# The second bias of the experts, added from a broadcast row by VectorE instead of a product on TensorE

## The chip, the cores and the metric

One core of one Trainium2 chip runs the kernel. The metric is the device time of one execution in microseconds (us), the median of several runs. Five engines work side by side and meet only at semaphores: TensorE (PE), VectorE (DVE), ScalarE (ACT), GpSimd (POOL) and SyncE (SP), which here only issues transfers.

## The reference, cut to what matters

4096 tokens of 256 features pass a graph layer over a 4096 x 4096 adjacency and then a mixture of 16 experts, of which each token uses two:

```python
h = gelu(xf @ W1[e] + b1[e])          # 256 -> 512
o = h @ W2[e] + b2[e]                 # 512 -> 256
y = y + combine[:, e:e + 1] * o       # combine: the token's weight for expert e
```

## The kernel before

**Stages.** A first stage loads and normalises the tokens (to about 54 us of the profile). A second goes through 32 tiles of 128 tokens: adjacency times features on TensorE, the graph layer, the router, and two rows per token (features, token number, weight) written to a list in DRAM that is sorted by expert (to about 380 us). The third stage, which the change is about, takes that list in `BLOCKS` = 79 blocks of 128 rows, each block of one expert, and adds the results to the output in DRAM.

**A step of the third stage.** Every engine runs its own `bstep(q, r)` for block b = 8q + r, in a fixed order, and works on different blocks at once:

- PE: `hidden(b)` (6 products of 512 columns, L530), `tokens_T(b+1)` (4 transposes, L510), `hidden_T(b-1)` (4 transposes, L538), `expert_out(b-2)` (L547 and 12 products of 256 columns, L553).
- DVE: `copy_tokens_T(b+1)` (L1032), `bias1(b)` (L1041), `cut_low(b-1)` (L1047), `weigh(b-2)` (L1055), and in odd steps of the first 32 `cut_low_late` (L1062).
- ACT: `gelu(b)` (L709), `cut_high(b-1)` (L715), and in odd steps of the first 32 `cut_high_late` (L705).
- SP: in odd steps `load_late` (L382, 512 KB of weights), then `load_block(b+4)` (L377, 136 KB of rows).
- POOL: `add_results(b-2)` (L1231, an indirect transfer that adds to the output).

Products are made in fp16 with every factor cut in a high and a low part. The weights of experts 0 to 7 are cut during the second stage; those of experts 8 to 15 are the 16 "late" halves, cut in the odd steps of blocks 1 to 31: ACT writes the high part, then DVE, which waits for it, the low part. SP waits for that low part before it loads the next weights into the same buffer.

**The second bias** is one more product at the head of `expert_out`: its stationary operand is a column of `sel`, broadcast, that picks expert e, and its moving operand is `b2hl`, which holds the high parts of all 16 biases in 16 partitions and the low parts in 16 others. `b2hl` and `sel` are made once in the first stage: a load on SP, a memset and a cut on DVE (L771, L814), a copy on ACT (L669), a memset and two selections on POOL (L1125, L1128), and one more transfer on SP (L352) ahead of its first weight load, which waits for the cut. `weigh` then multiplies by the token's weight while it copies out of PSUM.

Of the kernel before, what the change touches and what calls it, by code (L numbers as in the profile page):

```python
# [37 lines left out]
P = 128  # L38
N = 4096
D = 256  # L40
E = 16
# [40 lines left out]
def build(nc, x, adj, gnn_W, gnn_b, Wr, br, W1, b1, W2, b2, out):  # L82
    ctx = ExitStack()

    def sb(name, shape, dt):
        return ctx.enter_context(nc.sbuf_tensor(name, shape, dt))

    def sem(name):
        return ctx.enter_context(nc.semaphore(name))
# [40 lines left out]
    brb = sb("brb", [P, E], F32)  # L130
    b2s = orows[0:E, 6, :]
    b2l = orows[0:E, 3, :].bitcast(F16)[:, 0:D]
    b2hl = sb("b2hl", [P, D], F16)
    sel = sb("sel", [P, E], F16)
    id32 = sb("id32", [P, P], F32)
# [90 lines left out]
    a_in = [sem(f"a_in{k}") for k in range(AB)]  # L226
    w_in = [sem(f"w_in{k}") for k in range(2)]
    w_late = [sem(f"w_late{k}") for k in range(2)]
    listed = [sem(f"listed{c}") for c in range(2)]
# [22 lines left out]
    def load_x(eng, c, b):  # L252
# [4 lines left out]
              (wr[:, :, :], Wr.rearrange("(c p) n -> p c n", p=P)),  # L257
              (b2s, b2),
              (gb, gnn_b.rearrange("(a d) -> a d", a=1).broadcast_to([P, D])),
# [62 lines left out]
    def _(sp):  # L322
# [20 lines left out]
        def step(i, k):  # L343
            t = tile(i, k)
            if is_(t, lambda t: 3 <= t < T + 3):
                store_base(i, k - 3)
            if isinstance(t, int) and t == T:
                load_b1()
            if isinstance(t, int) and t == 0:
                sp.wait_ge(ev("b2_cut"), 1)  # L350
                after(sp, "b2_zeros", 0)
                sp.dma_start(b2hl[E:2 * E, :], b2l).then_inc(ev("b2_in"), 16)  # L352
            if k % 2 == 0 and is_(t, lambda t: t < T):
                which = k // 2
                if is_(i, lambda i: i >= 1):
                    sp.wait_ge(ev("w_cut"), i * 2 + which - 1)
                sp.dma_start(staged(which, which), w_dram(i, which)).then_inc(w_in[which], 16)
# [26 lines left out]
        AHEAD = 4  # L384

        def bstep(q, r):
            if late(q, r) is not None and late(q, r) + 2 < 2 * (E - EARLY):
                load_late(late(q, r) + 2)
            nxt = shift(q, r, AHEAD)
            if exists(*nxt):  # L390
                load_block(*nxt)
# [13 lines left out]
    def _(pe):  # L405
# [135 lines left out]
        def expert_out(q, r):  # L541
            e = expert[r] if r < U - 2 else expert_of(q, r)
            after(pe, "low_cut", blk(q, r))
            if not isinstance(q, int) or blk(q, r) >= 2:
                after(pe, "weighted", blk(q, r) - 2)
            n = 0
            pe.matmul(q_o[r % 2][:, 0:D], sel[:, bass.ds(e, 1)].broadcast_to([P, P]), b2hl[:, :], start=True, stop=False)  # L547
            for c in range(HC):
                high, low = hh[:, r % 2, c * P:(c + 1) * P], hl[:, r % 2, c * P:(c + 1) * P]
                wh = wall[:, bass.ds(w_at(e, 1, 0) + c * D, D)]  # L550
                wl = wall[:, bass.ds(w_at(e, 1, 1) + c * D, D)]
                for a, w in ((high, wh), (high, wl), (low, wh)):
                    mm = pe.matmul(q_o[r % 2][:, 0:D], a, w, start=False, stop=n == 3 * HC - 1)  # L553
                    n += 1
            mm.then_inc(ev("expert_out"), 1)
# [11 lines left out]
        pe.wait_ge(ev("table_made"), 1)  # L567
        pe.wait_ge(ev("b2_in"), 16)
        pe.wait_ge(ev("sel_made"), 3)
        tokens_T(0, 0)  # L570
# [16 lines left out]
    def _(act):  # L587
# [34 lines left out]
        def scale_base(i, k):  # L622
            r = tile(i, k)
            if is_(r, lambda r: r >= 2):
                act.wait_ge(base_out[k % 2], pair(i, k) * 16)
            if isinstance(r, int) and r < 2:
                act.wait_ge(ev("b2_in"), 16)
            after(act, "base_scale", r)
            after(act, "base_shift", r)
            act.activation(base[k % 2], x1, ACT.Identity, scale=bs[:, 0:1], bias=bs[:, 1:2]).then_inc(ev("base_made"), 1)  # L630
# [36 lines left out]
        act.activation(wg[:, 0, :, :], wg_arrival, ACT.Copy, scale=SW).then_inc(ev("wg_high"), 1)  # L667
        after(act, "b2_zeros", 0)
        act.activation(b2hl[0:E, :], b2s, ACT.Copy, scale=SW).then_inc(ev("b2_high"), 1)  # L669

# [40 lines left out]
        def cut_high(q, r):  # L711
# [3 lines left out]
            act.activation(hh[:, r % 2, :], q_g[r % 2][:, :], ACT.Copy, scale=SH).then_inc(ev("high_cut"), 1)  # L715

        def bstep(q, r):
            prev = shift(q, r, -1)
            if exists(q, r):
                gelu(q, r)  # L720
            if exists(*prev):
                cut_high(*prev)
            if late(q, r) is not None:
                cut_high_late(late(q, r))
# [5 lines left out]
    def _(dve):  # L730
# [39 lines left out]

        V.memset(b2hl[:, :], 0.0).then_inc(ev("b2_zeros"), 1)  # L771
        V.memset(gb_ones[:, :], SX * SW / 2.0 / SG / (P // 2)).then_inc(ev("gb_ones"), 1)
# [25 lines left out]
        for c in range(1, XC):  # L798
# [13 lines left out]
                               op0=ALU.mult, op1=ALU.subtract).then_inc(ev("gb_cut"), 1)  # L812
        after(V, "b2_high", 0)
        V.scalar_tensor_tensor(out=b2l, in0=b2s, scalar=SW, in1=b2hl[0:E, :],  # L814
                               op0=ALU.mult, op1=ALU.subtract).then_inc(ev("b2_cut"), 1)

# [232 lines left out]

        def weigh(q, r):  # L1050

            after(V, "expert_out", blk(q, r))
            if not isinstance(q, int) or q > 0:
                after_added(V, q - 1, r)
            V.tensor_scalar(orow[r], q_o[r % 2][:, 0:D], info[r][:, 1:2].bitcast(F32), None, ALU.mult)\  # L1055
             .then_inc(ev("weighted"), 1)

# [9 lines left out]
        def bstep(q, r):  # L1067
            prev, prev2, nxt = shift(q, r, -1), shift(q, r, -2), shift(q, r, 1)
            if exists(q, r):
                e = expert_of(q, r)  # L1070
            if exists(*nxt):
                copy_tokens_T(*nxt)
            if exists(q, r):
                bias1(q, r, e)
            if exists(*prev):
                cut_low(*prev)
            if exists(*prev2):
                weigh(*prev2)
            if late(q, r) is not None:
                cut_low_late(late(q, r))  # L1080
# [5 lines left out]
    def _(pool):  # L1086
# [37 lines left out]
        L.iota(pad[:, D:D + 1].bitcast(I32), [[0, 1]], base=N, channel_multiplier=1).then_inc(ev("pad_made"), 1)  # L1124
        L.memset(sel[:, :], 0.0).then_inc(ev("sel_made"), 1)  # L1125
        for k in range(2):
            L.wait_ge(ev("sel_made"), 1 + k)
            L.affine_select(out=sel[:, :], in_=sel[:, :], compare_op=ALU.not_equal, fill=SH, base=-E * k,  # L1128
                            pattern=[[-1, E]], channel_multiplier=1).then_inc(ev("sel_made"), 1)

        def rstd0(c):
# [139 lines left out]
```

## Time and profile before

| | |
|---|---|
| median of 3 runs | 705.9 us (705.65 to 708.77) |
| the profiled execution, time | 704.46 us |
| its span (first to last instruction) | 702.5 us |
| granted clock of TensorE, mean over the span | 0.971 |
| PE, DVE, ACT, POOL busy | 83%, 69%, 33%, 51% |

The span is what the trace covers; 1.96 us of the profiled execution lie around it. Busy shares are means over stages with different limits, so they don't say which engine sets a stage's pace.

### The profile page before, as it was taken

The numbers are of one execution on the slowest core, as the hardware profiler recorded it, in microseconds if no ns is written. First come the engines' busy times: TensorE is split into PE (matmuls) and PEld (weight loads), VectorE is DVE, ScalarE is ACT, GpSimd is POOL, SyncE is SP. The second block draws the span as 40 slices with busy tenths as digits, with TensorE's granted clock in tenths as the row PEclk, the third lists the DMA queues.
The fourth block names the chain that finished last, engine by engine and source line by source line (L and its number), as shares of the span: only waits on it lengthen the run. The fifth ranks groups of instructions, "written<-read, shape, count | busy, mean of one in ns | idle before, by whom it ended". The sixth has DMA issues, their size and how long they took to land.

```text
span 702.5 us, 17495 instructions
## 1 busy us (share of the span) xinstructions
PE 585.0 (83%) x4798; PEld 454.3 (65%) x4799; DVE 486.3 (69%) x1430; ACT 229.1 (33%) x440; POOL 361.8 (51%) x392
## 2 busy tenths in 40 slices
PE   0009999999999999999972479999999999999993
PEld 0007888788887788788862156666667677776772
DVE  2794788888888888888875156766665555555552
ACT  2260323333333332333322034443443233232331
POOL 4473367566675666666435734444443444444444
PEclk9999999999999999999995599999999999999997
DMA  9549688899888888899254335676654444444420
GB/s 266 112 73 192 117 162 180 184 178 185 169 181 179 154 170 176 182 183 182 82 170 172 133 105 124 132 152 145 134 107 77 77 76 70 66 73 68 75 41 0
DMA packets 65915, 93.21 MB, mean 133 GB/s; under 512 B 9547, under 2 KB 40559, under 8 KB 65360
## 3 DMA queue, kind: packets, MB, share of 16 engines
q0 software_dynamic: 33696, 51.87, 44.5%
q1 hardware_dynamic: 31024, 38.72, 17.4%
q10 hardware_dynamic: 1152, 2.10, 0.9%
q8 instruction: 21, 0.34, 0.2%
q14 instruction: 22, 0.18, 0.1%
HBM read 103.71 MB, written 25.83 MB: 184 GB/s over the span
## 4 chain that ended last, share of the span: by engine, by line
PE 40%; DVE 29%; issue 18%; POOL 6%; DMA 2%; DVEq 2%; ACT 2%; POOLq 1%; SPq 0%; ACTq 0%
PE bank L530 13%; PE bank L553 13%; DVE at_xg L781 7%; PE bank L538 4%; PE bank L510 2%; DVE wall L839 2%; DVE bst L849 2%; DVE orows L846 2%; POOL rows L1216 2%; PE bank L473 2%; PE bank L421 2%; PE bank L475 2%; DVE xf L865 1%; DVE xseT L832 1%; PE bank L547 1%
## 5 line engine op out<-in xcount | busy, mean ns | idle before, releaser
L473 PE MATMUL bank<-wall,at_xg 128*128 128x257 f16 x1024 | 238.1, 275 | 0.0
L475 PE MATMUL bank<-wall,at_xg 128*128 128x256 f16 x1024 | 237.9, 275 | 0.0
L1231 POOL DMA_INDIRECT out_dram<-orows,at_xg x79 | 125.1, 1584 | 164.5 <-DMA out_dram<-orows,at_xg 113.5
L530 PE MATMUL bank<-wall,feat 128*128 x474 | 117.0, 383 | 10.0 <-issue 8.0
L1047 DVE SCALAR_TENSOR_TENSOR wg<-bank,xseT 128x512 f16<-128x512 f32 x79 | 54.6, 691 | 92.2 <-ACT xseT L715 92.2
L473 PEld LDWEIGHTS bank<-wall,at_xg 128*128 128x128 f16 x1024 | 103.6, 101 | 13.3
L475 PEld LDWEIGHTS bank<-wall,at_xg 128*128 128x128 f16 x1024 | 100.9, 99 | 13.3
L709 ACT ACTIVATE hgs<-hgs 128x512 f32<-128x512 f32 x79 | 49.8, 630 | 181.7 <-DVE hgs L1041 181.7
L553 PE MATMUL bank<-wall,xseT 128*128 x632 | 108.1, 273 | 0.0
L781 DVE STREAM_TRANSPOSE at_xg<-abuf 128x512 int32<-128x512 int32 x128 | 89.4, 699 | 20.3 <-DMA abuf<-in_adj_dram 10.5
L1197 POOL DMA_INDIRECT rows<-feat,posi x64 | 68.2, 1066 | 50.1 <-issue 49.7
L553 PE MATMUL bank<-wall,wg 128*128 x316 | 86.1, 273 | 0.0
L530 PEld LDWEIGHTS bank<-wall,feat 128*128 128x128 f16 x474 | 46.1, 98 | 57.8 <-issue 23.4
L248 POOL DMA_DIRECT2D abuf<-in_adj_dram x128 | 72.7, 584 | 11.2 <-DVE at_xg L781 9.3
L1184 POOL TENSOR_TENSOR feat<-xf,feat 128x512 f16<-128x512 f32 x32 | 37.2, 1161 | 73.0 <-ACT feat L619 73.0
L553 PEld LDWEIGHTS bank<-wall,xseT 128*128 128x128 f16 x632 | 61.7, 98 | 8.5
L1041 DVE SCALAR_TENSOR_TENSOR hgs<-bank,abuf 128x512 f32<-128x512 f32 x79 | 53.7, 680 | 0.0
L1032 DVE COPY feat<-bank 128x512 f16<-128x512 f16 x79 | 33.3, 422 | 25.8 <-PE bank L510 23.9
L619 ACT ACTIVATE feat<-xf 128x512 f16<-128x512 f32 x32 | 20.2, 631 | 94.3 <-DVE xf L865 88.8
L538 PE MATMUL bank<-id,hgs 128*128 128x128 f32 x316 | 48.0, 274 | 0.7 <-ACT hgs L709 0.7
L715 ACT ACTIVATE xseT<-bank 128x512 f16<-128x512 f32 x79 | 45.8, 579 | 0.3 <-PE bank L538 0.3
L502 PE MATMUL bank<-firsts,ones 128*128 128x16 f16 x1 | 0.2, 173 | 54.3 <-DVE gbm L811 54.3
(153 smaller groups left out, 835.9 us busy)
## 6 DMA issues: line engine op xcount, KB each, us to landing
abuf<-in_adj_dram POOLq DMA_DIRECT2D x128, 256.0 KB, 6.0
wst<-in_L_ffn_W_dram SPq DMA_DIRECT2D x32, 512.0 KB, 4.8
at_xg<-rows SPq DMA_DIRECT2D x79, 136.0 KB, 2.4
out_dram<-orows SPq DMA_DIRECT2D x32, 128.0 KB
abuf<-in_L_ffn_b_dram SPq DMA_DIRECT2D x4, 1024.0 KB, 10.5
wall<-in_x_dram ACTq DMA_DIRECT2D x8, 256.0 KB, 8.8
wall<-in_x_dram SPq DMA_DIRECT2D x8, 256.0 KB, 8.0
out_dram<-orows,at_xg POOLq DMA_INDIRECT x79
```

The lines of the kernel that those rows point to most:

```text
L248: eng.dma_start(arrived[b * PQ:(b + 1) * PQ, k % AB, :, :], adj_v[bass.ds(pair(i, k), 1), k % 2, b, :, :, :].rearrange("n i a c -> i (n a) ...
L473: both = [lambda: pe.matmul(ps_acc[odd][:, 0:D + 1], w, xh[:, j, 0:D + 1], start=j == 0, stop=j == T - 1), lambda: pe.matmul(ps_acc[odd][: ...
L475: lambda: pe.matmul(ps_acc[odd][:, 0:D], w, xl[:, j, :], start=False, stop=False)]
L530: mm = pe.matmul(q_h[r % 2][:, :], a, w, start=n == 0, stop=n == 3 * DC - 1)
L538: mm = pe.transpose(q_g[r % 2][:, c * P:(c + 1) * P], hg[r % 2][:, c * P:(c + 1) * P], id32[:, :])
L553: mm = pe.matmul(q_o[r % 2][:, 0:D], a, w, start=False, stop=n == 3 * HC - 1)
L709: act.activation(hg[r % 2], hg[r % 2], ACT.Gelu).then_inc(ev("gelued"), 1)
L781: V.transpose(at[:, c, :].bitcast(I32).rearrange("p (n a i) -> p a n i", a=Q, i=PQ), arrived[:, k % AB, :, c * CW // CH:(c + 1) * CW // CH ...
L1041: V.scalar_tensor_tensor(out=hg[r % 2], in0=q_h[r % 2][:, :], scalar=1.0 / (SX * SW), in1=b1all[:, bass.ds(e * H, H)], op0=ALU.mult, op1=A ...
L1047: V.scalar_tensor_tensor(out=hl[:, r % 2, :], in0=q_g[r % 2][:, :], scalar=SH, in1=hh[:, r % 2, :], op0=ALU.mult, op1=ALU.subtract).then_i ...
L1197: L.indirect_dma_start(rows, at_place, feat[:, odd, k, :], None).then_inc(listed[odd], 16)
L1231: L.indirect_dma_start(out, bass.IndirectOffsetOnAxis(ap=info[r][:, 0:1].bitcast(U32), axis=0), orow[r], None, bounds_check=N - 1, oob_is_ ...
```

## The change

PE's bias product, `sel` and `b2hl` go, with all that made them. SP gets `load_b2(b-1)` at the head of its step b: it reads the block's expert from the table, waits until `summed` of block b-3 is there (the buffer is one of two) and loads that expert's row of `b2` from DRAM into all 128 partitions, 128 KB in SBUF. DVE's `weigh` becomes `add_b2`: it waits for the row and adds it, scaled, to PE's result on its way out of PSUM. The weight is now applied by ACT, in place, in a new `weigh(b-2)` that stands in ACT's step behind `cut_high(b-1)` and ahead of `cut_high_late`. PE waits for `summed` instead of `weighted` before it reuses a bank; POOL still waits for `weighted`.

```diff
-    b2s = orows[0:E, 6, :]
-    b2l = orows[0:E, 3, :].bitcast(F16)[:, 0:D]
-    b2hl = sb("b2hl", [P, D], F16)
-    sel = sb("sel", [P, E], F16)
+    b2row = [feat[:, k, 1, 0:D] for k in range(2)]
...
-              (b2s, b2),
...
-            if isinstance(t, int) and t == 0:
-                sp.wait_ge(ev("b2_cut"), 1)
-                after(sp, "b2_zeros", 0)
-                sp.dma_start(b2hl[E:2 * E, :], b2l).then_inc(ev("b2_in"), 16)
...
+        def load_b2(q, r):
+
+            e = sp.value_load(tab[0:1, bass.ds(blk(q, r) + P, 1)], min_val=0, max_val=E - 1)
+            if not isinstance(q, int) or blk(q, r) >= 2:
+                after(sp, "summed", blk(q, r) - 2)
+                passed(sp)
+            sp.dma_start(b2row[r % 2], b2[bass.ds(e, 1), :].broadcast_to([P, D])).then_inc(b2_in[r % 2], 16)
+
         def bstep(q, r):
+            if exists(*shift(q, r, -1)):
+                load_b2(*shift(q, r, -1))
...
-                after(pe, "weighted", blk(q, r) - 2)
+                after(pe, "summed", blk(q, r) - 2)
             n = 0
-            pe.matmul(q_o[r % 2][:, 0:D], sel[:, bass.ds(e, 1)].broadcast_to([P, P]), b2hl[:, :], start=True, stop=False)
...
-                    mm = pe.matmul(q_o[r % 2][:, 0:D], a, w, start=False, stop=n == 3 * HC - 1)
+                    mm = pe.matmul(q_o[r % 2][:, 0:D], a, w, start=n == 0, stop=n == 3 * HC - 1)
...
-            if isinstance(r, int) and r < 2:
-                act.wait_ge(ev("b2_in"), 16)
...
-        act.activation(b2hl[0:E, :], b2s, ACT.Copy, scale=SW).then_inc(ev("b2_high"), 1)
...
+        def weigh(q, r):
+
+            after(act, "summed", blk(q, r))
+            act.activation(orow[r], orow[r], ACT.Copy, scale=info[r][:, 1:2].bitcast(F32)).then_inc(ev("weighted"), 1)
+
         def bstep(q, r):
-            prev = shift(q, r, -1)
+            prev, prev2 = shift(q, r, -1), shift(q, r, -2)
             if exists(q, r):
                 gelu(q, r)
             if exists(*prev):
                 cut_high(*prev)
+            if exists(*prev2):
+                weigh(*prev2)
             if late(q, r) is not None:
                 cut_high_late(late(q, r))
...
-        V.memset(b2hl[:, :], 0.0).then_inc(ev("b2_zeros"), 1)
...
-        V.scalar_tensor_tensor(out=b2l, in0=b2s, scalar=SW, in1=b2hl[0:E, :],
-                               op0=ALU.mult, op1=ALU.subtract).then_inc(ev("b2_cut"), 1)
...
-        def weigh(q, r):
+        def add_b2(q, r):
 
             after(V, "expert_out", blk(q, r))
+            V.wait_ge(b2_in[r % 2], (q * (U // 2) + r // 2) * 16 + 16)
             if not isinstance(q, int) or q > 0:
                 after_added(V, q - 1, r)
-            V.tensor_scalar(orow[r], q_o[r % 2][:, 0:D], info[r][:, 1:2].bitcast(F32), None, ALU.mult)\
-             .then_inc(ev("weighted"), 1)
+            V.scalar_tensor_tensor(out=orow[r], in0=b2row[r % 2], scalar=SH * SW, in1=q_o[r % 2][:, 0:D],
+                                   op0=ALU.mult, op1=ALU.add).then_inc(ev("summed"), 1)
...
-        L.memset(sel[:, :], 0.0).then_inc(ev("sel_made"), 1)
-        for k in range(2):
-            L.wait_ge(ev("sel_made"), 1 + k)
-            L.affine_select(out=sel[:, :], in_=sel[:, :], compare_op=ALU.not_equal, fill=SH, base=-E * k,
-                            pattern=[[-1, E]], channel_multiplier=1).then_inc(ev("sel_made"), 1)
```

## Rows read from the trace of the kernel before

**Rows 1.** The page's first part: busy time, share of the span, instructions.

```profile
PE 585.0 (83%) x4798; PEld 454.3 (65%) x4799; DVE 486.3 (69%) x1430; ACT 229.1 (33%) x440; POOL 361.8 (51%) x392
```

**Rows 2.** Windows of the third stage: length, busy us (instructions) per engine, clock, DMA share, GB/s.

```profile
404.00:412.00 8.00, 3.72 (x27) 2.49 (x28) 3.78 (x6) 2.63 (x5) 2.36 (x3) 1.00 0.23 55
...
426.00:518.00 92.00, 86.22 (x660) 60.08 (x657) 63.16 (x111) 38.11 (x60) 40.44 (x26) 1.00 0.64 140
518.00:680.00 162.00, 158.69 (x1233) 114.13 (x1231) 97.15 (x185) 52.24 (x93) 71.28 (x46) 1.00 0.42 72
```

**Rows 3.** Timeline of DVE, ACT and SP, two steps: start, duration, instruction, idle before.

```profile
460.33 0.68 DVE L1041 SCALAR_TENSOR_TENSOR hgs<-bank,abuf 128x512 f32<-128x512 f32 x1
...
461.05 0.63 ACT L709 ACTIVATE hgs<-hgs 128x512 f32<-128x512 f32 x1 [2.08 <-DVE hgs L1041]
...
461.58 0.58 ACT L715 ACTIVATE xseT<-bank 128x512 f16<-128x512 f32 x1
...
462.06 1.05 ACT L705 ACTIVATE wall<-wst 128x1024 f16<-128x1024 f32 x1
462.19 0.69 DVE L1047 SCALAR_TENSOR_TENSOR wg<-bank,xseT 128x512 f16<-128x512 f32 x1 [1.18 <-ACT xseT L715]
462.80 0.47 DVE L1055 TENSOR_SCALAR orows<-bank,at_xg 128x256 f32<-128x256 f32 x1
...
463.19 1.21 DVE L1062 SCALAR_TENSOR_TENSOR wall<-wst,wall 128x1024 f16<-128x1024 f32 x1
...
464.43 0.39 SPq L382 DMA_DIRECT2D wst<-in_L_ffn_W_dram  x1
...
464.66 0.68 DVE L1041 SCALAR_TENSOR_TENSOR hgs<-bank,abuf 128x512 f32<-128x512 f32 x1
...
466.26 2.22 SPq L377 DMA_DIRECT2D at_xg<-rows  x2
...
470.32 0.47 DVE L1055 TENSOR_SCALAR orows<-bank,at_xg 128x256 f32<-128x256 f32 x1
...
470.71 1.21 DVE L1062 SCALAR_TENSOR_TENSOR wall<-wst,wall 128x1024 f16<-128x1024 f32 x1
```

**Rows 4.** Groups by line from 380 us: count, busy and mean, idle and releaser.

```profile
L1062 DVE SCALAR_TENSOR_TENSOR wall<-wst,wall 128x1024 f16<-128x1024 f32 x16 | 19.4, 1213 | 0.3 <-ACT wall L705 0.3
```

**Rows 5.** Timelines of PE and of DVE in a late step.

```profile
560.49 0.27 PE L547 MATMUL bank<-b2hl,sel 128*128 128x256 f16 x1
560.60 0.38 PE L553 MATMUL bank<-wall,xseT 128*128 x2
...
563.72 0.43 DVE L1032 COPY feat<-bank 128x512 f16<-128x512 f16 x1 [0.18 <-PE bank L510]
```

**Rows 6.** Window with L530 alone, PE's six products of each block: busy (count).

```profile
518.00:680.00 162.00, 67.39 (x276) 26.69 (x276) 1.00 0.42 72
```

**Rows 7.** Lines L650 and L666 of ACT: ns min/median/max, first and last start.

```profile
L650 ACT ACTIVATE wall<-wall,shift,rstd x17: 583/584/599, 12.9 to 43.7; 128x256 f32<-128x256 f32 x17
...
L666 ACT ACTIVATE gbm<-orows x1: 400/400/400, 46.2 to 46.2; 128x256 f16<-128x256 f32 x1
```

**Rows 8.** Line L377 of SP from 452 to 484 us, with issue to landing.

```profile
L377 SPq DMA_DIRECT2D at_xg<-rows x9: 332/333/341, 455.4 to 483.9; - x9
...
DMA to landing us min/median/max: 2.1/2.1/3.8
```

**Rows 9.** Timeline of the end.

```profile
692.73 0.48 DVE L1055 TENSOR_SCALAR orows<-bank,at_xg 128x256 f32<-128x256 f32 x1 [1.44 <-PE bank L553]
...
695.02 1.56 POOL L1231 DMA_INDIRECT out_dram<-orows,at_xg  x1 [0.63 <-issue]
```

**Rows 10.** First stage: timeline of POOL and DVE, and a DMA issue with us to landing.

```profile
5.51 0.54 POOL L1128 TENSOR_SCALAR_AFFINE_SELECT sel<-sel 128x16 f16<-128x16 f16 x2
...
21.31 0.71 DVE L781 STREAM_TRANSPOSE at_xg<-abuf 128x512 int32<-128x512 int32 x1 [10.46 <-DMA abuf<-in_adj_dram]
...
orows<-in_L_ffn_b_dram SPq DMA_DIRECT2D x1, 16.0 KB, 15.9
```

More of the change, by code:

```diff
@@ L227, in build @@
     w_in = [sem(f"w_in{k}") for k in range(2)]
+    b2_in = [sem(f"b2_in{k}") for k in range(2)]
     w_late = [sem(f"w_late{k}") for k in range(2)]
@@ L567, in _ @@
         pe.wait_ge(ev("table_made"), 1)
-        pe.wait_ge(ev("b2_in"), 16)
-        pe.wait_ge(ev("sel_made"), 3)
         tokens_T(0, 0)
@@ L667, in _ @@
         act.activation(wg[:, 0, :, :], wg_arrival, ACT.Copy, scale=SW).then_inc(ev("wg_high"), 1)
-        after(act, "b2_zeros", 0)
-        act.activation(b2hl[0:E, :], b2s, ACT.Copy, scale=SW).then_inc(ev("b2_high"), 1)
         def step(i, k):
@@ L812, in _ @@
                                op0=ALU.mult, op1=ALU.subtract).then_inc(ev("gb_cut"), 1)
-        after(V, "b2_high", 0)
-        V.scalar_tensor_tensor(out=b2l, in0=b2s, scalar=SW, in1=b2hl[0:E, :],
-                               op0=ALU.mult, op1=ALU.subtract).then_inc(ev("b2_cut"), 1)
         def pool_x(s, odd):
@@ L1077, in bstep @@
             if exists(*prev2):
-                weigh(*prev2)
+                add_b2(*prev2)
             if late(q, r) is not None:
```

## The prediction, made before the changed kernel ran

> **What bounds the kernel now.** I read the page's busy shares first [rows 1]: PE 83%, DVE 69%. These mix three stages, so I split the third by windows [rows 2]. From 518 us on, PE is busy 158.69 of 162 us and DVE 97.15: PE sets the pace. From 426 to 518 us PE is busy 86.22 of 92, DVE 63.16; no engine is full, so there I read the timeline [rows 3].
>
> The timeline shows a closed loop between DVE and ACT. `bias1` (L1041) runs 460.33 to 461.01; `gelu` (L709) starts at 461.05 on its release; `cut_high` (L715) follows on ACT until 462.16; `cut_low` (L1047), which waited 1.18 us for it, starts at 462.19; then `weigh` (L1055) at 462.80, the late cut (L1062) at 463.19, and the next `bias1` at 464.66. No DVE row there waits for PE. One late cut to the next is 470.71 - 463.19 = 7.52 us for two steps. PE's own work for two steps is less. In the late stage a step takes 162 us / (276 / 6) = 3.52 us [rows 6], 7.04 for two, and there a DVE row does wait for PE (L1032, 0.18 us for the transposes of L510) [rows 5]. So before about 525 us the DVE-ACT loop is the limit, after it PE. The chain of waits names PE nearly everywhere in both stages because it is followed backwards through PE's queue; the rows of DVE, which never waits for PE in the early stage, are what I go by.
>
> **PE's product removed.** L547 starts at 560.49 and the next product at 560.60 [rows 5]: it holds the array 0.11 us, not the 0.27 of its row, since products overlap. In the DVE-ACT stage this buys nothing. In the late stage there are 276 / 6 = 46 blocks [rows 6] x 0.11 = 5.1 us. At the starts of the unrolled loop's rounds, two steps in eight, I don't know that PE's array is the limit; without those it is 34 x 0.11 = 3.7. I take **-4.4** (3.7 to 5.1). DVE does not take over there: `bias1` to `bias1` in a step with a late cut is 464.66 - 460.33 = 4.33 [rows 3], and without the cut, whose share is its 1.21 less the overlap with its follower, about 3.2, under the 3.4 left to PE.
>
> **DVE's instruction.** `add_b2` reads PSUM and SBUF and writes 128x256 like L1055 (0.47) [rows 3]; I take 0.48 and no change.
>
> **ACT's new instruction, and what is queued behind it.** This is the main term. No row shows a 256-element ACT copy out of SBUF with one per-partition operand. L666 with none takes 0.400 us, L650 with two takes 0.584 [rows 7]; I take the middle, 0.49. Its 79 x 0.49 = 39 us of work would be harmless on an engine with 33% load [rows 1]. But ACT takes its queue in order, and `weigh(b-2)` waits for DVE's `summed(b-2)`, which DVE makes after `cut_low(b-1)`. Behind it in ACT's odd steps stands `cut_high_late`, and for that DVE waits before its own late cut.
>
> Today L705 starts at 462.06, right behind L715, and ends at 463.11 while DVE does L1047 and L1055; L1062 starts at 463.19, 0.39 us after L1055 [rows 3]. All 16 late cuts together wait 0.3 us for ACT [rows 4]. After the change the order from the start of DVE's add is serial:
> - the add, 0.48;
> - to ACT, 0.04 (461.01 to 461.05);
> - `weigh`, 0.49, its follower starting 0.10 before its end (L709 ends at 461.68, L715 starts at 461.58);
> - L705, 1.05;
> - to DVE, 0.03 (462.16 to 462.19).
>
> That is 0.48 + 0.04 + 0.49 - 0.10 + 1.05 + 0.03 = 1.99 instead of 0.39: **1.60 us later** (1.51 with 0.400, 1.69 with 0.584). Nothing covers it, as DVE stands in its queue ahead of the next `copy_tokens_T`, `bias1`, so of `gelu`, `cut_high`, and of PE's next `hidden`. The pair of steps goes from 7.52 to 9.12 us. Of the 16 late cuts the first, in step 1, has no `weigh` ahead of it (block -1 doesn't exist): 15 x 1.60 = **+24.0** (22.7 to 25.4).
>
> One pair in the stage is stretched today by a late block load. I give back 0.5 us for it, an allowance: **-0.5** (0 to -1).
>
> In steps without a late cut `weigh` costs nothing: it ends about 0.48 + 0.04 + 0.49 = 1.01 us after the add starts. The next `gelu` waits for a `bias1` whose end, with L1032 in between (0.43 [rows 5]) and 0.68 of its own, is 0.39 + 0.34 + 0.68 = 1.41 after it. If ACT's instruction took over 0.9 us, that cover would be gone.
>
> **SP's new transfer.** It moves 128 KB per block, 128 pieces of 1 KB. SP has room: two block loads start 2.22 - 0.33 = 1.89 us apart [rows 3, 8] against a step of over 3.4, and `load_b2` has about half their table reads, about 1 us. Its wait for `summed(b-3)` is met a step earlier. What may be late is its landing, in the cut stage. The cut ends at 464.40; SP issues 512 KB of weights at 464.43, a block load at 466.26, and would issue the row about 467.5 [rows 3]. DVE wants it at 470.32, the next odd add; the stretch of 1.60 lies behind that add, so this distance stays. Block loads land 2.1 us after issue at best and 3.8 at worst [rows 8]; a row would be there at 469.6 to 471.3, 0.7 early to 1.0 late. The loads behind a weight load are the slow ones and the row stands behind both, so I take 0.15 us late in 14 pairs: **+2** (0 to +14). Even rows are issued a step earlier relative to their use.
>
> The spread between 2.1 and 3.8 is what the Trainium skill's page "DMA: Bandwidth & Descriptors", section "Queues, rings and completion order", would lead one to expect: the descriptors of one issuing queue are taken in order, so a small row waits behind 512 KB. The same page's section "Anatomy of one DMA" prices a transfer at 2.0 us plus bytes over 436 GB/s, 2.3 us here; by that alone the row is on time and the sum is 2 us lower.
>
> **First stage.** POOL's two selections and memset go, so its first adjacency loads are issued up to 0.54 us sooner, and DVE's first transpose waits for them (10.46 us) [rows 10]. The DMA engines are loaded then; **-0.3** (0 to -0.6). DVE's and ACT's bias cut lie beside longer waits, 0. SP's first two weight loads (1 MB) no longer wait for the bias cut and are issued at some 7 us instead of 55. They stand behind SP's own constants, which need 15.9 us to land [rows 10], about when that transpose starts: 0, at worst 3.5 us if they share the engines with the adjacency (1 MB at some 300 GB/s, an estimate).
>
> **The end.** The last add ends at 693.21 and POOL issues at 695.02 [rows 9]; ACT now stands between: **+0.5** (0.4 to 0.6).
>
> **TensorE's clock.** PE idles more in the cut stage. It was granted 1.00, the 2.4 GHz level, through 404 to 412 us with PE busy 3.72 of 8 us [rows 2]; the new stage keeps it busier, so 0.
>
> **Sum.** 24.0 - 0.5 - 4.4 + 2.0 - 0.3 + 0.5 = +21.3 us. On the profiled execution that is 702.5 + 1.96 + 21.3 = 725.8; the median stands 1.4 above that execution (705.9 against 704.46), so **727 us**, 3% slower.
>
> **The rivals.**
> 1. *The row is late as well.* DVE waits for `b2_in` in most odd steps, near the slow end of the bound: 1.0 us x 14 instead of 2, +12, so 739 us. For it: 64% DMA load in that stage [rows 2], and the row's place behind weights. Against it: half the block loads there land in 2.1 us [rows 8].
> 2. *The cover holds* (the other side). If the late cuts' chain is not what sets the pair's 7.52 us, then only PE's gain counts: 705.9 - 4.4 - 0.3 + 0.5 = 701.7. It decides at the point where ACT's late copy is done by the time DVE has ended its add; that needs `cut_high_late` to start about 1.1 us before `summed`, which the order in ACT's queue forbids, or 1.6 us of slack on DVE, of which the rows show none. A hidden slack at the loop of PE's queue is the only way that I see.
> 3. *Partly covered*: PE's early `hidden` lets DVE catch up with half of the 1.60: +9.3, so 715.
>
> **Chances.** Forecast 0.75, its own range 722 to 733; rival 1 0.13; rival 2 0.08; rival 3 0.04. The sums of the low and the high ends are 22.7 - 1 - 5.1 + 0 - 0.6 + 0.4 = +16.4 (722) and 25.4 - 3.7 + 14 + 3.5 + 0.6 = +39.8 (746). The range leaves out rival 2 and most of rival 3 and goes three quarters of the way to the high end: 719 to 740. A change under 0.5% (3.5 us) can't be told from none here. Faster takes most of rival 2: 0.07; within it 0.03; slower 0.90.
>
> **What would show it.** In the changed profile: late cuts (L1062's successor) 9.1 us apart, with about 1.5 us idle before each of 15, released by ACT's late copy, 22 to 24 us in all; ACT's late copy waiting behind `weigh`; `weigh` near 0.49 us; PE steps of some 3.28 us where they were 3.39; little or no DVE idle put down to the row's transfer. The prediction is wrong if the late cuts' idle stays under 0.5 us each, or if idle time released by the `b2` transfer adds over 5 us.

## The result: 743.8 us, 5.3% slower

| | before | after |
|---|---|---|
| median | 708.0 us (6 runs beside those of after) | 743.8 us (6 runs, 743.5 to 747.9) |
| ratio to before, 95% interval | | 1.0526 [1.0494, 1.0557] |
| profiled execution / its span | 704.46 / 702.5 us | 743.81 / 742.2 us |

The direction is as forecast, the size is not: 743.8 us lies above the range (719 to 740). The forecast was +21.3 us on the profiled execution; it is +39.7 us on the span. Of the cases that I wrote down, rival 1 (the row is late as well, 739 us) is the nearest, and it too is short.

The page of after, its busy times and the shares of the chain that ended last:

```profile
PE 587.0 (79%) x4719; PEld 448.0 (60%) x4720; DVE 484.3 (65%) x1428; ACT 268.8 (36%) x518; POOL 364.9 (49%) x389
...
DVE 30%; issue 21%; DMA 21%; PE 8%; POOL 6%; ACT 5%; SPq 4%; DVEq 2%; POOLq 1%; ACTq 0%
```

Against [rows 1], PE has 79 instructions fewer, ACT 78 more and 39.7 us more work; DVE's work is the same within 2 us. No engine's busy share became full, so the time is in waits. (SP's queue, for which the page has no busy share, did fill up; that comes below.)

**Where it went.** I cut the third stage at PE's first `hidden` product of blocks 0, 32 and 78. In after these are, from three stretches of PE's timeline:

```profile
395.36 1.03 PE L533 MATMUL bank<-wall,feat 128*128 x2 [0.81 <-DVE feat L1031]
...
550.01 0.82 PE L533 MATMUL bank<-wall,feat 128*128 x3 [0.60 <-issue]
...
723.16 1.03 PE L533 MATMUL bank<-wall,feat 128*128 x4
```

and in before the same product starts at 398.22, 522.45 and 684.85. The differences give the table, with what the prediction's terms gave for the same stretch:

| stretch | before | after | measured | predicted |
|---|---|---|---|---|
| up to block 0 | 398.2 | 395.4 | -2.9 | -0.3 |
| block 0 to 32 (the late cuts) | 124.2 | 154.7 | +30.4 | 24.0 - 0.5 + 2.0 = +25.5 |
| block 32 to 78 (the late stage) | 162.4 | 173.1 | +10.7 | -4.4 |
| block 78 to the end | 17.6 | 19.1 | +1.4 | +0.5 |
| sum | 702.5 | 742.2 | +39.7 | +21.3 |

So the error of 18.4 us is 4.9 in the stretch that I had worked on hardest and 15.1 in the one where I had expected a gain, less 1.7 in the two others.

These are lengths in one profile of each kernel. Before has the shortest first stretch of all: e6 to e9 below, which are all as fast as before or faster, have 125.3 to 127.2 there. From block 0 to 415 us before was granted a clock of 0.90, after 0.67 and the ten kernels below 0.64 to 0.83, whether they have the change or not. Up to some 3 of the 30.4 us may be that and not the change.

**The stretch of the late cuts.** The groups of after by line, from 380 us on: count, busy and mean, idle time before and its releasers. L1062 answers to [rows 4].

```profile
L716 ACT ACTIVATE orows<-orows,at_xg 128x256 f32<-128x256 f32 x79 | 40.1, 508 | 102.1 <-DVE orows L1055 101.1 <-issue 1.1
L1055 DVE SCALAR_TENSOR_TENSOR orows<-feat,bank 128x256 f32<-128x256 f32 x79 | 32.7, 413 | 15.2 <-DMA feat<-in_L_ffn_b_dram 13.6 <-PE bank L555 1.5
L1062 DVE SCALAR_TENSOR_TENSOR wall<-wst,wall 128x1024 f16<-128x1024 f32 x16 | 19.6, 1225 | 23.1 <-ACT wall L701 23.1
```

The late cut now waits 23.1 us for ACT's late copy where it waited 0.3. The same two steps as in [rows 3], in the timeline of DVE, ACT and SP of after:

```profile
457.04 1.23 DVE L1062 SCALAR_TENSOR_TENSOR wall<-wst,wall 128x1024 f16<-128x1024 f32 x1 [1.52 <-ACT wall L701]
...
460.13 0.33 SPq L370 DMA_DIRECT2D at_xg<-rows  x1
...
461.27 0.33 SPq L385 DMA_DIRECT2D feat<-in_L_ffn_b_dram  x1
...
462.90 0.58 ACT L711 ACTIVATE xseT<-bank 128x512 f16<-128x512 f32 x1
463.06 0.33 SPq L370 DMA_DIRECT2D at_xg<-rows  x1
463.51 0.69 DVE L1046 SCALAR_TENSOR_TENSOR wg<-bank,xseT 128x512 f16<-128x512 f32 x1 [1.18 <-ACT xseT L711]
...
464.69 0.42 DVE L1055 SCALAR_TENSOR_TENSOR orows<-feat,bank 128x256 f32<-128x256 f32 x1 [0.49 <-DMA feat<-in_L_ffn_b_dram]
465.15 0.51 ACT L716 ACTIVATE orows<-orows,at_xg 128x256 f32<-128x256 f32 x1 [1.67 <-DVE orows L1055]
465.56 1.04 ACT L701 ACTIVATE wall<-wst 128x1024 f16<-128x1024 f32 x1
466.63 1.23 DVE L1062 SCALAR_TENSOR_TENSOR wall<-wst,wall 128x1024 f16<-128x1024 f32 x1 [1.52 <-ACT wall L701]
```

To be seen: ACT has ended `cut_high` (L711) at 463.48 and could make its late copy (L701) then, as it did before. It stands idle for 1.67 us instead, for `weigh` (L716) is ahead in its queue and waits for DVE's add (L1055), which itself waits 0.49 us for the row. While the copy is made DVE has nothing else to do, and the late cut starts after 1.52 us of waiting. One cut to the next is 466.63 - 457.04 = 9.59 us: the 9.12 of the prediction and the 0.49 of the row.

**The late stage.** DVE and SP of after around blocks 53 and 54, from the two engines' timelines:

```profile
634.18 0.33 SPq L385 DMA_DIRECT2D feat<-in_L_ffn_b_dram  x1
637.61 0.33 SPq L370 DMA_DIRECT2D at_xg<-rows  x1
638.84 0.33 SPq L385 DMA_DIRECT2D feat<-in_L_ffn_b_dram  x1
640.89 0.33 SPq L370 DMA_DIRECT2D at_xg<-rows  x1
...
641.86 0.42 DVE L1055 SCALAR_TENSOR_TENSOR orows<-feat,bank 128x256 f32<-128x256 f32 x1 [0.46 <-DMA feat<-in_L_ffn_b_dram]
642.26 0.33 SPq L385 DMA_DIRECT2D feat<-in_L_ffn_b_dram  x1
643.14 0.42 DVE L1031 COPY feat<-bank 128x512 f16<-128x512 f16 x1 [0.85 <-issue]
...
646.19 0.42 DVE L1055 SCALAR_TENSOR_TENSOR orows<-feat,bank 128x256 f32<-128x256 f32 x1 [0.15 <-DMA feat<-in_L_ffn_b_dram]
```

The row issued at 638.84 is the one that the add at 641.86 waits for, and the row issued at 642.26 the one of the add at 646.19. DVE's add is late here too, with no late cut in the neighbourhood. What waited from 550 to 720 us (us in total, times, longest):

```profile
DVE orows L1055 <- DMA feat<-in_L_ffn_b_dram: 6.4, 9, 1.5
DVE feat L1031 <- issue: 6.2, 14, 0.9
...
DVE wall L1062 <- ACT wall L701: 1.5, 1, 1.5
```

The second row is a follow-on. A DVE step begins with the table read for `bias1`; while DVE ran ahead of its data that read lay inside a wait, and where an add is late, the copy behind it shows it as "issue" idle; in e2 and e3 below, where no add waits for a row there, it is 0.2 us. The third is the last late cut, which falls into this stretch. The three together are 14.1 us. Less the 2.8 us that the missing PE product turned out to be worth here (e7 below) that is 11.3, against 10.7 measured.

Why the row is late there is mostly in SP's queue. SP issues the row behind the block load of the step before, and that load waits until the addition of an earlier block has landed, which needs that block's add, `weigh` and POOL. So an add that is late makes a row late, whose add is four blocks on. The load at 637.61 had waited 1.4 us in this way, and the row behind it went out 2.6 us before the add was ready, where 3.6 us is usual. Of the nine late rows seven were issued right behind such a wait; the other two, that of 642.26 among them, were issued in time and took 3.8 and 4.6 us to land. SP's waits in before, 523 to 684 us, and in after, 550 to 720 us:

```profile
SPq L221 <- DMA out_dram<-orows,at_xg: 65.3, 39, 2.8
```

```profile
SPq L218 <- DMA out_dram<-orows,at_xg: 17.6, 13, 3.7
```

SP used to reach the block load early and to wait for the addition in 39 of the steps, 65.3 us in all. That was its slack; 17.6 us of it are left. In the cut stage a block load follows the last one after 463.06 - 460.13 = 2.93 us with the row between them, where it was 1.89: the row takes 1.04 us of SP's step, as the prediction said. In the late stage it takes more. From 550.11 to 716.70 us SP issues 43 block loads after the first, so its own part of a step, without these waits, is (166.6 - 17.6) / 43 = 3.5 us, where in before it is about 2.1. PE's shortest step is 3.28. SP has nothing to spare there, so a row once late stays late. This alone costs nothing as long as no engine waits for the row: SP's part is as long in e6 below, which is as fast as before.

### The profile page after: what moved, and what is told of

Read it like the earlier page. It is cut to its first block, busy times and chain, and to the rows that moved or that the text cites. A ratio compares the mean times of both kernels' runs of the same rounds, so it can differ in the third digit from the quotient of the medians.

```text
span 742.2 us, 17974 instructions
## 1 busy us (share of the span) xinstructions
PE 587.0 (79%) x4719; PEld 448.0 (60%) x4720; DVE 484.3 (65%) x1428; ACT 268.8 (36%) x518; POOL 364.9 (49%) x389
## 3 DMA queue, kind: packets, MB, share of 16 engines
HBM read 114.05 MB, written 25.83 MB: 188 GB/s over the span
## 4 chain that ended last, share of the span: by engine, by line
DVE 30%; issue 21%; DMA 21%; PE 8%; POOL 6%; ACT 5%; SPq 4%; DVEq 2%; POOLq 1%; ACTq 0%
DMA out_dram<-orows,at_xg 12%; DVE at_xg L783 7%; DMA feat<-in_L_ffn_b_dram 6%; DVE wall L1062 2%; ACT wall L701 2%; DVE wall L838 2%; DVE bst L848 2%; DVE orows L845 2%; POOL rows L1210 2%; DMA rows<-feat,posi 1%; PE bank L476 1%; PE bank L478 1%; PE bank L424 1%; DVE xf L864 1%; PE bank L533 1%
## 5 line engine op out<-in xcount | busy, mean ns | idle before, releaser
L1225 POOL DMA_INDIRECT out_dram<-orows,at_xg x79 | 128.9, 1631 | 202.9 <-DMA out_dram<-orows,at_xg 137.3
L533 PE MATMUL bank<-wall,feat 128*128 x474 | 120.5, 392 | 45.5 <-DVE feat L1031 30.9
L555 PE MATMUL bank<-wall,xseT 128*128 x632 | 109.6, 275 | 6.5 <-DVE wg L1046 6.3
L716 ACT ACTIVATE orows<-orows,at_xg 128x256 f32<-128x256 f32 x79 | 40.1, 508 | 102.1 <-DVE orows L1055 101.1
L1031 DVE COPY feat<-bank 128x512 f16<-128x512 f16 x79 | 33.3, 422 | 30.9 <-PE bank L513 23.5
L711 ACT ACTIVATE xseT<-bank 128x512 f16<-128x512 f32 x79 | 45.7, 579 | 0.0
```

Of the source, the lines that this page charges most:

```text
L533: mm = pe.matmul(q_h[r % 2][:, :], a, w, start=n == 0, stop=n == 3 * DC - 1)
L555: mm = pe.matmul(q_o[r % 2][:, 0:D], a, w, start=n == 0, stop=n == 3 * HC - 1)
L1225: L.indirect_dma_start(out, bass.IndirectOffsetOnAxis(ap=info[r][:, 0:1].bitcast(U32), axis=0), orow[r], None, bounds_check=N - 1, oob_is_ ...
```

## The experiments

Ten kernels. Ratios are to before in runs on the same chip, with the 95% interval; they, not the us, compare one row with another. The lengths of stretches are of one profiled execution each and cut as above.

| | what | us | ratio | block 0 to 32 | 32 to 78 |
|---|---|---|---|---|---|
| | before | 708.0 | 1 | 124.2 | 162.4 |
| | after | 743.8 | 1.0526 [1.0494, 1.0557] | 154.7 | 173.1 |
| e1 | late copy ahead of `weigh` | 724.3 | 1.0246 [1.0214, 1.0279] | 136.6 | 169.5 |
| e2 | rows of blocks 0 and 1 only | 725.4 | 1.0268 [1.0233, 1.0302] | 146.6 | 162.7 |
| e3 | rows two steps earlier | 727.9 | 1.0290 [1.0254, 1.0327] | 146.2 | 167.0 |
| e4 | e1 and e3 | 714.3 | 1.0110 [1.0067, 1.0152] | 134.0 | 162.9 |
| e5 | before, with loads nobody reads | 714.9 | 1.0132 [1.0088, 1.0175] | 133.2 | 163.2 |
| e6 | e5 into 16 partitions | 706.6 | 0.9996 [0.9980, 1.0013] | 126.7 | 162.5 |
| e7 | before, without the PE product | 702.9 | 0.9941 [0.9919, 0.9964] | 125.3 | 159.6 |
| e8 | before, PE's table read earlier | 707.3 | 0.9996 [0.9981, 1.0011] | 127.1 | 162.6 |
| e9 | e1 and e2 | 702.4 | 0.9929 [0.9905, 0.9953] | 127.2 | 161.5 |
| e10 | e4, rows one step later | 710.5 | 1.0044 [1.0017, 1.0072] | 136.7 | 162.3 |

**e1: the order in ACT's queue.** The change with two calls swapped.

```diff
-            if exists(*prev2):
-                weigh(*prev2)
             if late(q, r) is not None: ... cut_high_late ...
+            if exists(*prev2):
+                weigh(*prev2)
```

> The changed kernel with ACT's weigh moved behind its late copy in the odd steps; nothing else. Theory: the 15 late cuts that stand 1.5 us idle each for ACT's late copy (23.1 us in all) are due to this order alone, so they go and the time falls by about 20 us, to 722 to 726, with the rows' lateness left (13.6 us of DVE idle put down to the row's transfer, perhaps more of it in the early stage, where the steps shorten). Rival, the row's transfer sets the early stage as well: then DVE only waits for the row instead and the time falls by less than 10 us, to 734 or more.

724.3 us: the swap alone gives back 19.5 us. Groups of DVE in e1 from 400 us:

```profile
L1055 DVE SCALAR_TENSOR_TENSOR orows<-feat,bank 128x256 f32<-128x256 f32 x79 | 32.7, 414 | 17.7 <-DMA feat<-in_L_ffn_b_dram 13.4 <-DMA out_dram<-orows,at_xg 2.5 <-PE bank L555 1.5
L1062 DVE SCALAR_TENSOR_TENSOR wall<-wst,wall 128x1024 f16<-128x1024 f32 x16 | 19.5, 1220 | 0.3 <-ACT wall L701 0.3
```

The late cut's wait is back at 0.3 us; `weigh` still runs 79 times on ACT. So ACT's new work costs nothing here, its place in the queue did. The add's wait for the row, 13.4 us, is untouched: a cause of its own, and the two don't lie in the same time. The stretch up to block 32 shortens by 154.7 - 136.6 = 18.1, less than the 21.5 us of the late cuts' wait that lie in it, for the rows came later relative to their use: there the add's wait for them rose from 7.2 to 9.7 us and the bared table read from 0.2 to 1.4.

**e2: no row to wait for.** The change, but only the first two rows are loaded; the second biases of later blocks are left out.

```diff
-            if exists(*shift(q, r, -1)):
-                load_b2(*shift(q, r, -1))
+            if isinstance(q, int) and q == 0 and 1 <= r <= 2:
+                load_b2(0, r - 1)
...
-            V.wait_ge(b2_in[r % 2], (q * (U // 2) + r // 2) * 16 + 16)
+            V.wait_ge(b2_in[r % 2], 16)
```

> The changed kernel, but SP loads rows for blocks 0 and 1 only, and every block adds one of these two (so the later biases are left out of the computation). ACT's order stays as changed. Theory: from block 32 on the row's transfer is what costs 15 us against the sum (waits of DVE, and what they expose behind them), so the late stage falls from 3.76 us a step to 3.3 to 3.45, and the early one loses 7 us; together 722 to 726. Rival, the late stage is slow by ACT's new instruction between DVE and POOL, or by the unrolled loop's own instruction loads: then the late stage stays above 3.65 us a step and the time above 733.

725.4 us: without transfers the change is 18 us shorter, 10.4 of it in the late stage (173.1 to 162.7), which is then as long as before, though PE's product is gone; the wait of the last late cut, 1.5 us, is still in it. In e2 the late cuts still wait 23.1 us. The removal takes three things at once: the wait, SP's time and the bytes. The next runs part them.

**e3: the row earlier.** Four row buffers instead of two, and the row of block b + 1 issued in step b instead of that of b - 1.

```diff
+    b2more = sb("b2more", [P, 2, D], F32)
-    b2row = [feat[:, k, 1, 0:D] for k in range(2)]
+    b2row = [feat[:, k, 1, 0:D] for k in range(2)] + [b2more[:, k, :] for k in range(2)]
...
-                after(sp, "summed", blk(q, r) - 2)
+                after(sp, "summed", blk(q, r) - 4)
...
-                load_b2(*shift(q, r, -1))
+                load_b2(*shift(q, r, 1))
```

> The changed kernel with four row buffers instead of two, so that SP issues the row of block b+1, not of block b-1, in its step b: two steps sooner, with the same traffic. Theory (the row lands late because it stands behind the wait for a block's landed addition): DVE's waits for the row go, 722 to 728. Rival, the added 10 MB of traffic slows the other transfers whenever it comes: then no more than 5 us are won, 739 or more.

727.9 us: 15.9 us of e2's 18.3 come back with every byte still moved. No wait of the add for a row is left in this profile. The late stage gains 6.2 us (173.1 to 167.0), not all of 10.4.

**e4: both.** The two diffs above together.

> Both: ACT's weigh behind the late copy, and the row two steps sooner. If the two causes are separate and complete, the time is that of before less the 5 us of PE's product and 1 to 3 us of the first stages: 699 to 704. If traffic or ACT's place between DVE and POOL costs by itself, it stays at 706 to 715.

714.3 us. Groups of DVE in e4 from 400 us:

```profile
L1064 DVE SCALAR_TENSOR_TENSOR wall<-wst,wall 128x1024 f16<-128x1024 f32 x16 | 19.6, 1225 | 0.3 <-ACT wall L703 0.3
L1057 DVE SCALAR_TENSOR_TENSOR orows<-feat,bank 128x256 f32<-128x256 f32 x40 | 16.4, 410 | 0.5 <-PE bank L557 0.5
L1057 DVE SCALAR_TENSOR_TENSOR orows<-b2more,bank 128x256 f32<-128x256 f32 x39 | 16.0, 411 | 2.3 <-PE bank L557 2.3
```

Both waits that the change had made are gone, and yet the kernel is 1.1% slower than before, the second of the two cases expected. Most of what is left lies ahead of block 32: 134.0 us where before has 124.2. The late stage is at 162.9, as in before, and so lacks the gain from PE's product (159.6 in e7).

**e5, e6: the bytes by themselves.** The kernel before, with the change's row transfer added at the same place of SP's queue, and no engine that reads it (only SP's next load into the same buffer waits for it, and its profile shows no such wait). In e6 the same instruction fills 16 partitions instead of 128.

```diff
+            if exists(*shift(q, r, -1)):
+                load_b2(*shift(q, r, -1))     # waits "weighted", not "summed"
...
-            sp.dma_start(b2row[r % 2], b2[bass.ds(e, 1), :].broadcast_to([P, D])).then_inc(b2_in[r % 2], 16)
+            sp.dma_start(b2row[r % 2][0:16, :], b2[bass.ds(e, 1), :].broadcast_to([16, D])).then_inc(b2_in[r % 2], 16)
```

(the first pair of lines for both, the last for e6.)

> The kernel before with SP's loads of the rows added at the same place and with the same wait (weighted in place of summed), into memory that nobody reads; nobody but SP's own next load waits for them. PE's product stays. Theory (with both waits mended a rest of some 10 us stayed in the early stage, where DVE then stands behind PE and PE behind late block loads): the 10 MB of traffic and SP's longer queue cost 6 to 12 us by themselves, nearly all before block 32: 713 to 719. Rival: what stayed came from ACT's instruction between DVE and POOL; then the loads alone cost under 3 us.

> As the run before, with each row loaded into 16 partitions instead of 128: the same instructions and waits on SP, an eighth of the bytes. If it is the bytes (the DMA engines' time), the cost falls to an eighth, under 2 us; if it is SP's queue, it stays within 2 us of the full loads.

e5 is 1.3% slower, e6 is equal to before. SP issues the same number of transfers and reads the table as often in both, so SP's time is not it; the size of the row in SBUF is. (Its bytes and its pieces of 1 KB fall together, 128 to 16, and no run parts these two.) The pages also show what is read from DRAM: 114.07 MB in e5, 105.01 in e6 and 103.71 in before, so 10.4 MB more in e5, which is 79 x 128 KB. The row of 1 KB is read once for every partition. DMA issues from 420 to 520 us, in before, in e5 and in e6 (count, KB, median us to landing):

```profile
wst<-in_L_ffn_W_dram SPq DMA_DIRECT2D x12, 512.0 KB, 3.9
```

```profile
wst<-in_L_ffn_W_dram SPq DMA_DIRECT2D x13, 512.0 KB, 4.6
```

```profile
wst<-in_L_ffn_W_dram SPq DMA_DIRECT2D x13, 512.0 KB, 3.5
```

and what PE waited for from 410 to 535 us, in the same order (total, times, longest):

```profile
PEld bank L510 <- DMA at_xg<-rows: 6.0, 3, 3.9
```

```profile
PEld bank L525 <- DMA at_xg<-rows: 12.8, 7, 4.4
```

```profile
PEld bank L525 <- DMA at_xg<-rows: 5.0, 3, 3.2
```

The rows, which nobody in e5 waits for, make the weights land later and the transposes (L510, L525 in e5 and e6) wait 12.8 us for block loads instead of 6.0 and 5.0. That is most of what this stretch grows by: 9.0 us against before, 6.4 against e6 (126.7 to 133.2). The late stage grows by 0.8 only, which one profile of each doesn't tell from chance. Every kernel has one wait of 3.0 to 4.8 us for a block load at 408 to 411 us, which falls into this window in before, e5 and e6 but not in after and e4. Without it the waits are 2.0 us in before, 1.8 in e6, 8.4 in e5, 14.5 in e4 and none in after, where DVE and ACT are so late that the block loads have time. These waits are weaker evidence than the times, for they differ between kernels without the transfers too: 0.9 in e7, 7.0 in e9. So the bytes' cost was hidden behind the other two, and came out as they were mended. e4 against e9 below, which differ by the transfers, gives their price once more, 1.0110 against 0.9929.

**e7: the gain by itself.** The kernel before without the product of L547; the second bias is left out.

> The kernel before without the bias product on PE (the second bias is left out of the computation); all else stays. The prediction's term says 0.11 us for each of 46 late blocks, 3.7 to 5.1 us less. The theory formed since (PE's queue reads the block's expert from a table behind expert_out's last product, and the products in flight are the cover of that read) says: under 1.5 us less, with PE's idle time before hidden grown by what the product took.

702.9 us, 4.2 us less than before in the ratio (0.0059 x 707): the prediction's term holds, and the under 1.5 us expected here does not. In the profile the late stage is 2.8 us shorter, its shortest step 3.28 instead of 3.39, which is the 0.11 us of the two starts in [rows 5]. But the mean of its 34 ordinary steps falls from 3.46 to 3.40 only. L530's idle time from 530 to 680 us, in before and in e7:

```profile
  issue: 10.7, 35
```

```profile
  issue: 14.9, 48
```

Part of the gain goes into idle time ahead of the next `hidden`, put down to "issue": it is likely that PE's sequencer hasn't yet read the expert from the table, which e8 looks at. The other 1.4 us can't be placed: e7's profile is 1.3 us shorter than before's ahead of block 0, where the product isn't at work, and 1.0 longer from there to block 32, which one profile of each doesn't tell from chance.

**e8: is PE's table read the limit?** The kernel before, where PE reads a block's expert from the table right behind the `hidden` of the block before, instead of just ahead of its own `hidden`.

```diff
+            if exists(q, r + 1) and r + 1 < U:
+                expert[r + 1] = expert_of(q, r + 1)
```

> The kernel before, with PE's table read of the next block's expert moved from before hidden(b+1) to right behind hidden(b), in seven of eight steps; nothing left out. If that read is what stretches late steps from 3.39 to 3.47 us, the late stage loses 0.05 to 0.1 us in each of 46 steps, 2 to 5 us; if not, nothing.

0.9996: no gain. In the profile L532 (before's L530) loses most of its idle time, 4.4 us in 9 waits are left, and from 593.25 to 606.77 us each `hidden` starts 3.38 us after the last with no idle time of PE before it. The last two of these steps and the next:

```profile
600.01 1.46 PE L532 MATMUL bank<-wall,feat 128*128 x6
...
603.39 1.46 PE L532 MATMUL bank<-wall,feat 128*128 x6
...
606.77 1.46 PE L532 MATMUL bank<-wall,feat 128*128 x6
...
610.65 1.47 PE L532 MATMUL bank<-wall,feat 128*128 x6 [0.33 <-issue]
```

The step that follows is 3.88. The steps in which the unrolled loop goes round take 3.92 us on average, 3.75 in before: what the ordinary steps gain is lost there. I haven't found out to what.

**e9: the change with neither cost.** The diffs of e1 and e2 together, so the second biases of blocks 2 and on are left out.

> The changed kernel with ACT's weigh behind its late copy and with rows loaded for blocks 0 and 1 only (the later biases are left out of the computation): what DVE's add and ACT's weigh cost with the right order and without traffic. Theory (order, lateness of the row and its bytes are the whole loss): the same as the kernel before without the product, 701 to 705. Rival, ACT between DVE and POOL costs by itself 3 us or more (the late stage of the run with rows once took 162.7 us, that without the product 159.6): 706 to 709.

702.4 us, 0.9929, the same as e7 within the intervals. Here DVE's add and ACT's `weigh` run in all 79 blocks. So with the right order and no transfers the two new instructions cost nothing that can be measured (the intervals are 3 us wide), and the PE product's 0.6% is what the change had to win. The stretches of e9 are longer than e7's because its profiled execution was the longest of six (704.6) and e7's the shortest (701.6).

**e10: another lead for the rows.** e4 with `load_b2` moved behind the block load in SP's step. As the step repeats, the queue then has the same order (block, row, weights), and what differs is that each row is issued one step later, with its buffer free one step longer.

```diff
-            if exists(*shift(q, r, 1)):
-                load_b2(*shift(q, r, 1))
             if late(q, r) is not None ...: load_late(...)
             if exists(*nxt):
                 load_block(*nxt)
+            if exists(*shift(q, r, 1)):
+                load_b2(*shift(q, r, 1))
```

> As the run with both mended (ACT's order, four row buffers, 714.3 us), but in SP's step the row stands behind the weight load and the block load instead of ahead of them. If the rest of the early stage's loss (PE waiting for late block loads) comes from the row standing ahead of the block in SP's queue, 3 to 6 us go: 708 to 711. If it is the bytes, as the loads into 16 partitions say, under 2 us go: 712.5 or more.

710.5 us, 1.0044, which is in the range expected if the row's place ahead of the block load were the cause. The profile doesn't show that cause: PE still waits 15.2 us for block loads (14.5 in e4), and the two stretches together are 299.0 us against 296.9. The two intervals overlap a little, and this profiled execution (715.3) was longer than the median. That e10 is a little faster than e4 is likely; why is open.

## Why the prediction was wrong

**ACT's order: right, and right in size.** The main term was 24.0 us (22.7 to 25.4); the late cuts' idle time is 23.1, all released by L701: 15 waits of 1.52 us where I had 1.60, and the first one's 0.3. `weigh` took 0.508 us (0.49 taken from the middle of [rows 7]), the add 0.413 (0.48). The Trainium skill's page "ScalarE: Activation LUTs", section "What ACT_TABLE_LOAD costs", gives 186 ns plus 0.833 ns a column and 93 ns for a per-partition operand, an estimate of 0.492 us for this instruction; the trace has 3% more. e1 shows that it is the order, since it alone takes the wait away; the time falls by 19.5 us only, since rows are waited for in its place. The prediction's "never waits for PE", of DVE in that stage, was not quite so: there are two such waits in before from 420 to 530 us, 0.5 us in all, too little to matter.

**The step that failed: SP's new transfer.** The prediction said "What may be late is its landing, in the cut stage", and gave it +2, with SP said to have room. The prediction also named the sign of being wrong, over 5 us of idle time put down to the row: it is 13.6. Three things in that step were wrong.

- *Only in the cut stage.* The late stage had no term for it. It holds half of the add's waits (6.4 of 13.6 us) and the 6.2 us of table read that they bare: instead of -4.4 that stage was +10.7, 15.1 of the error's 18.4 us. I had set 1.89 us for a block load and 1 for the row against a step of 3.4, and SP's own part came out at 3.5. And I had looked at the wait for the row's buffer ("met a step earlier") and not at what stands ahead of the row in SP's queue: the block load's wait for a landed addition. That is the rule of the main term, an instruction that waits delays what is queued behind it, which I applied to ACT and not to SP. e2 and e3 show it: 10.4 and 6.2 us of the late stage go when the row isn't needed or is earlier.
- *The size in the cut stage.* 7.2 us in 13 waits rather than 2 in 14. The distance from issue to use was as forecast (some 2.9 us for an odd row, 2.8 forecast), the landing was not: 2.8 us at best and 3.2 in the median over the whole kernel. I had taken the row's time from the block loads of [rows 8], 2.1 at best, and weighed it towards that end. The page of after:

```profile
at_xg<-rows SPq DMA_DIRECT2D x79, 136.0 KB, 2.3
feat<-in_L_ffn_b_dram SPq DMA_DIRECT2D x79, 128.0 KB, 3.2
```

  The Trainium skill's page "DMA: Bandwidth & Descriptors", section "Anatomy of one DMA", gives 2.0 us plus bytes over 436 GB/s for a transfer issued by GpSimd, which would be 2.3 us for 128 KB, an estimate. The prediction took it for a row issued by SyncE; the median here is 0.9 above it, and the measurement decides. The traffic alone is not the reason, since the block loads, a little larger and from the same queue, land in 2.3. What differs in the row is that the same 1 KB is read 128 times; whether that is the reason isn't shown.
- *The bytes.* I priced what the row suffers from the other loads and not what the others suffer from it. e5 makes it 1.3%, 9.3 us, where it isn't hidden. In after itself it is: from 410 to 535 us PE's weight loads have no wait for a block load.

**PE's product: right in its sum, not in its place.** -4.4 (3.7 to 5.1), and e7 has -4.2 (-2.5 to -5.7, its interval times 707). But the late stage, where the whole term was put, accounts for 2.8, and its ordinary step shrank by 0.06 us and not by the 0.11 of the forecast. That the sum is so near is in part luck.

**What was to cost nothing cost nothing.** e9 confirms it for the add and for `weigh` outside the steps with a late cut. The one pair given back (-0.5) is too small to be told.

**The first stage** came out 2.9 us shorter where 0.3 was forecast. POOL's first adjacency load starts at 5.26 us, where it was 6.48, and DVE's first transpose at 20.71, 0.60 earlier than in [rows 10] and so at the end of the forecast's range. SP's first weight loads went out from 9.24 us, and the transpose was no later for it. The rest I can't give to the change: in the ten other kernels block 0 starts between 395.9 and 398.0 us.

**The end** was +1.4 instead of +0.5. From the last add to POOL's last issue it is 734.78 - 731.20 = 3.58 us instead of 695.02 - 692.73 = 2.29 [rows 9]. `weigh` explains its 0.5; the block before, whose addition POOL waits for (1.32 us), is the rest.

```profile
731.20 0.42 DVE L1055 SCALAR_TENSOR_TENSOR orows<-feat,bank 128x256 f32<-128x256 f32 x1 [1.46 <-PE bank L555]
731.65 0.51 ACT L716 ACTIVATE orows<-orows,at_xg 128x256 f32<-128x256 f32 x1 [1.37 <-DVE orows L1055]
732.54 1.56 POOL L1225 DMA_INDIRECT out_dram<-orows,at_xg  x1 [1.32 <-DMA out_dram<-orows,at_xg]
734.78 1.56 POOL L1225 DMA_INDIRECT out_dram<-orows,at_xg  x1 [0.68 <-issue]
```

**TensorE's clock** had 0, and that holds but for a few us at the start of the cut stage. Windows of after, columns as in [rows 2]:

```profile
404.00:412.00 8.00, 5.23 (x26) 3.32 (x25) 3.63 (x5) 2.66 (x5) 0.62 (x1) 0.74 0.32 72
426.00:550.00 124.00, 91.80 (x670) 61.50 (x667) 67.22 (x116) 54.34 (x91) 45.30 (x26) 0.99 0.59 135
550.00:720.00 170.00, 155.41 (x1171) 108.03 (x1172) 93.99 (x181) 73.76 (x137) 70.83 (x45) 1.00 0.53 100
```

In the cut stage PE is busy 91.80 of 124 us, 74%, where it was 94%, and is still granted 0.99. In the 8 us from 404 it was granted 0.74 of full speed, a mean of the two levels of 1.2 and 2.4 GHz, with about as many products as before (26 and 27); its busy time there rose from 3.72 to 5.23 us. The change isn't the reason: e6 and e7, which are before with small edits, were granted 0.64 and 0.66 from block 0 to 415 us, after 0.67.

**What stays open.** Whether the change can win at all with the biases right. The best version with it is e10, 0.4% over before. e9 bounds what could be had without transfers at -0.7%. All 16 rows kept in SBUF would need 16 KB in each partition; it wasn't tried, and whether there is room isn't shown.

## What to carry to other kernels

An instruction given to a lightly loaded engine costs its place in the queue rather than its time: look for what stands behind it while it waits. Do this for every queue that the change touches, the one that issues transfers too, and in every stage, and add up that queue's own time per step: here 23 us of waiting on ACT were foreseen, and 13.6 on SP's rows were not. A transfer beside others has two prices, its own lateness and that of the others, and the second may show only when the first is mended.

## What the runs showed of the hardware

- A row of 1 KB broadcast from DRAM into 128 partitions (128 KB) costs as 128 KB and not as 1 KB: the pages count 79 x 128 KB more read from DRAM in after and e5 (114.05 and 114.07 MB against 103.71). With 16 partitions instead of 128 and the same number of issues, the slowdown went from 1.3% to none (e5, e6).
- From the same queue and in the same kernel, such a row took 3.2 us to land in the median (2.8 at best) and a block load of 136 KB 2.3.
- A table read on an engine's sequencer is free while the engine is ahead and shows up to 0.85 us as "issue" idle once its data is late (L1031 in after). It couples waits: 6.4 us of late rows in the late stage brought 6.2 us of bared reads, which are 0.2 in e2 and e3.
- Taking 0.11 us of products out of a step whose array is the limit shortened the step by 0.06 on average (3.46 to 3.40), while PE's idle time ahead of the next `hidden` grew from 10.7 to 14.9 us (e7).
